# Second attention: the value products of the third group of heads placed in the next unit's list loop

## The reference, cut to what matters

```
x = _layernorm(x + _L0_attn_ref(x, ...))      # 32 heads of 128, sliding window
x = _layernorm(x + _L0_ffn_ref(x, ...))
x = _layernorm(x + _L1_attn_ref(x, ...))      # the part that changes
x = _layernorm(x + _L1_ffn_ref(x, ...))

# _L1_attn_ref: 32 query heads of 16 columns, 8 key heads, so 4 query heads share a key head
draft = einsum('bhqd,bhkd->bhqk', qr, kr) + causal mask
_, draft_indices = top_k(draft, 128)          # 128 largest keys of each query row and head
mask = neg everywhere, 0 at draft_indices, neg above the diagonal
scores = einsum('bhqd,bhkd->bhqk', qr, kr) / sqrt(16) + mask
out = einsum('bhqk,bhkd->bhqd', softmax(scores), v) @ Wo.T
```

## Time and profile before

| | us |
|---|---|
| median of three runs | 2230.96 |
| the profiled execution | 2229.73 |
| its span | 2227.9 |
| busy in the span: TensorE | 1843.1 (83%) |
| VectorE | 1500.7 (67%) |
| ScalarE | 1181.9 (53%) |
| GpSimd | 802.1 (36%) |

### The profile page before, as it was taken

The page is one execution under the profiler, slowest core; times in us unless marked ns, Lnnn a source line. Parts: engine busy times, 40 slices in busy tenths (PEclk is TensorE's granted clock), DMA queues, the critical chain, the costliest instruction groups (busy, mean ns, idle before and its releaser), DMA issues. The chain is left out here.

```text
span 2227.9 us, 27786 instructions
## 1 busy us (share of the span) xinstructions
PE 1843.1 (83%) x8586; PEld 1325.6 (60%) x8600; DVE 1500.7 (67%) x3316; ACT 1181.9 (53%) x2969; POOL 802.1 (36%) x519
## 2 busy tenths in 40 slices
PE   5899899998999869999766677777777778667997
PEld 4777777777777657888653343333333344436885
DVE  3677777777777654555754678888888887822345
ACT  3556556565565433332435676877667766342221
POOL 3445455454554425654411211112321111123442
PEclk9999999999999979999875888889888887787998
DMA  4011121111210112231221000010000000001111
GB/s 162 26 54 56 42 96 44 53 52 45 96 44 25 62 57 85 85 111 59 80 92 51 15 15 15 15 29 13 16 15 15 15 9 8 14 15 48 43 42 52
DMA packets 49490, 104.11 MB, mean 47 GB/s; under 512 B 6768, under 2 KB 31728, under 8 KB 45296
## 3 DMA queue, kind: packets, MB, share of 16 engines
q1 hardware_dynamic: 49392, 102.95, 13.6%
HBM read 95.59 MB, written 7.34 MB: 46 GB/s over the span
## 5 line engine op out<-in xcount | busy, mean ns | idle before, releaser
L230 PE MATMUL PS<-XT,AR 128*128 128x512 f32 x2472 | 621.5, 406 | 26.2 <-POOL AR L838 12.3
L230 PE MATMUL PS<-AR 128*128 128x512 f32 (+2 forms) x2568 | 540.0, 364 | 24.2 <-POOL AR L347 13.1
L230 PEld LDWEIGHTS PS<-XT,AR 128*128 128x128 f32 x2472 | 472.1, 193 | 140.2 <-issue 17.0
L230 PEld LDWEIGHTS PS<-AR 128*128 128x128 f32 x2568 | 440.9, 192 | 116.6 <-POOL AR L347 16.2
L1536 POOL TENSOR_TENSOR AF<-AF 128x1024 f32<-128x1024 f32 (+3 forms) x56 | 140.1, 2502 | 598.0 <-DVE AF L1811 598.0
L1753 DVE MAX8 BF<-PS 128x8 f32<-128x256 f32 (+2 forms) x384 | 196.6, 555 | 59.8 <-PE PS L1295 53.4
L1448 ACT ACTIVATE AF<-PS 128x512 f32<-128x512 f32 x152 | 87.5, 594 | 217.8 <-PE PS L1306 149.4
L1320 PE MATMUL PS<-AF,BF 128*128 128x512 f32 x304 | 175.8, 683 | 24.7 <-ACT AF L1448 24.6
L591 POOL TENSOR_TENSOR AF<-AF 128x512 f32<-128x512 f32 (+1 forms) x64 | 107.5, 1680 | 167.9 <-DVE AF L722 167.9
L585 POOL TENSOR_TENSOR AF<-AF 128x512 f32<-128x512 f32 x80 | 103.1, 1289 | 170.6 <-ACT AF L377 170.6
L558 ACT ACTIVATE AF<-AF 128x256 f32<-128x256 f32 (+1 forms) x256 | 120.3, 471 | 64.5 <-DVE AF L716 64.5
(11 more groups left out here) (213 smaller groups left out, 3484.1 us busy)
## 6 DMA issues: line engine op xcount, KB each, us to landing
AF<-in_mean_w SPq DMA_DIRECT2D x48, 448.0 KB, 3.3
AF<-in_ffn_w SPq DMA_DIRECT2D x14, 1536.0 KB, 6.5
AF<-in_attn_w SPq DMA_DIRECT2D x9, 1536.0 KB, 7.0
XT<-rope_scratch SPq DMA_DIRECT2D x174, 64.0 KB, 2.7
AF<-in_attn_w SPq DMA_DIRECT2D x9, 1024.0 KB, 5.2
AF<-in_ffn_w SPq DMA_DIRECT2D x11, 769.0 KB, 4.2
rope_scratch<-BF SPq DMA_DIRECT2D x20, 256.0 KB, 2.3
AF<-in_x SPq DMA_DIRECT2D x8, 256.0 KB, 4.3
```

Source lines behind the costliest of these rows:

```text
L230: last = nc.tensor.matmul(dst, lhs(a, c), rhs(m, c), start=(first and k == 0), stop=(k == 3 * n - 1 and not more))
```

## The change

On TensorE the value steps of group 2 leave the unit's own value phase (`q < 3` becomes `q < 2`) and stand in the next unit's list loop ahead of those of group 3: step s of the two groups together stands behind head s, for s from 0 to 2(i+2)-1. On ScalarE the copies of group 2 leave the end of the value phase, and the copies of both groups stand one before every two heads of the first count, in place of one before every four. On VectorE the first update stands behind head 8, where it stood behind head 6. The second update stays behind head 14.

```
@@ pe_attn1
-                    if 0 <= xp - 1 < NB and h <= tile_of(xp - 1)[1] + 1:
-                        values(xp - 1, 3, h)
+                    if 0 <= xp - 1 < NB:
+                        steps = tile_of(xp - 1)[1] + 2
+                        if h < 2 * steps:
+                            values(xp - 1, 2 + h // steps, h % steps)
...
-                    if 0 <= xp < NB and q < 3:
+                    if 0 <= xp < NB and q < 2:
                         for kb in range(tile_of(xp)[1] + 2):
                             values(xp, q, kb)
@@ act_attn1
-                for k in range(4):
-                    if 0 <= xp - 1 < NB and k <= tile_of(xp - 1)[1]:
-                        pt(xp - 1, 3, [k])
+                for k in range(8):
+                    if 0 <= xp - 1 < NB and k < 2 * (tile_of(xp - 1)[1] + 1):
+                        pt(xp - 1, 2 + k // (tile_of(xp - 1)[1] + 1), [k % (tile_of(xp - 1)[1] + 1)])
                     if search:
-                        count(x, 0, range(4 * k, 4 * k + 4))
+                        count(x, 0, range(2 * k, 2 * k + 2))
...
                     pt(xp, 1)
                     exp(xp, 3)
-                    pt(xp, 2)
@@ dve_attn1
-                    if search and h in (6, 14):
-                        update(x, (h - 6) // 8)
+                    if search and h in (8, 14):
+                        update(x, (h - 8) // 6)
```

## The result

The changed kernel takes 2299.74 us, the median of four runs (2295.11 to 2300.96), beside 2233.1 us for the kernel before on the same chip (2230.54 to 2236.7). The ratio is 1.0294, interval 1.0275 to 1.0313: slower by 66.6 us. I had forecast +48 us (2277) and a range up to 2296. Direction and most of the mechanism came out, the size did not, and one cost was missing from the sum.

What follows compares the result with a forecast made beforehand. List loops were taken as bound by TensorE for the first i+2 heads, then VectorE; value phases by VectorE's chain. 28.8 us for order plus 19 for clock on 2229.7 gave 2277.5, forecast 2277, range 2262 to 2292 (2252 to 2296 with rivals).

Steps and rivals of the forecast that it cites:

- Group 2 out of the value phase: 0.: Value phase: VectorE's chain ends it and needs no group 2, so nothing is won; TensorE only waits longer.
- The added steps and the chain through ScalarE.: List loops: 34 steps of 1.36 us and a later last copy delay both updates; unit 5's cut +4.0 us.
- the replay: Step-by-step timing of each list loop under the new order, giving unit 7 4.2 us and unit 10 3.
- The term of 28.8: Sum over the list loops of what the new order costs, without the clock: 28.8 us.
- Fewer copy waits: 1 to 1.3 us a loop.: List loops: with a copy before every two counts, products stop waiting for ScalarE's copies, worth 1 to 1.3 us a loop.
- Loops where a tile ends.: `o_lo` behind head 7 waits for the last product; VectorE stands 5.4 us in unit 6; loops +4.5 (unit 6), +6.9 (unit 8).
- rival 3: Low clock lasts two spells instead of one, another 3 us on six or seven loops: 2297 us; chance 0.12.
- The clock at the start: 19 us.: Longer waits ahead of the lists start nearly every list loop at the low clock: 19 us, bounds 0 and 36.
- Rival 2: List loops: the added steps fill TensorE's 36.3 us of waits for picks, so the kernel gets faster, 2222 us; chance 0.04.
- Rival 4: No change: slack behind head 9 hides the cost, units 3 to 8 lose under 1 us each, 2230 to 2237; chance 0.03.
- My argument against the page: Value phases of the kernel before: twelve restarts at low clock lose 12 x 3.3 = 40 us, 1.8% of the span.

Runs made afterwards that it cites:

- the shorter filling: Changed kernel plus 6(i+1) unread 128x512 matmuls on TensorE behind group 1 of the values, units 0 to 10: 2287.32 us; with `o_lo` behind head 10: 2265.73 us.
- the longer filling: Changed kernel with `o_lo` behind head 10 and 8(i+1) unread 128x512 matmuls behind group 1 of the values: 2256.74 us, ratio 1.0113.
- light steps: Changed kernel with group 2 cut to one transpose a step and products of 4 columns, copies full size: 2285.05 us, ratio 1.0253.
- the spread projection: Kernel before with filling matmuls ahead of the value phases and the projection split into four pieces behind heads 9 to 12: 2223.48 us, ratio 0.9962.

## Why the prediction failed in its size

The 66.6 us taken apart by the medians: with `o_lo` behind head 10 -17.5 (2282.2), with the clock up at every loop's start a further -25.5 (2256.7), and 23.9 are left. Taken each against the kernel before that was timed beside it, the parts are 20.3, 22.5 and 23.9 us. They also depend a little on the order: the shorter filling gave 12.4 us with `o_lo` behind head 7 and 16.5 us with it behind head 10.

- *Group 2 out of the value phase: 0.* Right. Value phases +1.4 us together; TensorE only waits longer for the first mark (71.5 us without unit 0, and I had said about 70).
- *The added steps and the chain through ScalarE.* Right in mechanism and about right in size. In unit 5's loop at full clock the price is 39.4 - 35.6 = 3.8 us; I had 4.0. In unit 3 it is 4.0 (I had 3.3), in unit 4 1.4 (0.9). In units 7 and 10 the replay does not fit: the loops are 0.7 us longer and 2.1 us shorter than before, where I had 4.2 and 3; but both started at a low clock in the kernel before, so their comparison is not at equal clock. The term of 28.8 also held the stand at `o_lo`; without it 23.9 us remain, and beside them stand the waits at the updates (30.5 us instead of 8.3).
- *Fewer copy waits: 1 to 1.3 us a loop.* The waits shrank (24.6 to 15.7 us), and alone this was worth nothing (ratio 1.0018); that the clock eats the gain fits units 6 and 8 but is not shown.
- *Loops where a tile ends.* **This is the step that failed.** I had the stand itself right (unit 6: forecast 5.4, measured 5.54), and said that the rest is "VectorE's own pace". It is not: behind the stand TensorE's clock falls a second time and the projection, 12 matmuls in a lump, runs into it. That added 9.3 us of waits in units 2, 4, 6 and 8 and was in no term of the sum. With the 4.8 us of stands in units 2, 4 and 10 (below) it covers the 12.5 us that these loops were over the forecast. It is the two spells of rival 3, to which I gave 0.12. TensorE did wait for picks, as rival 3 says, but for picks held up by `o_lo`, and the second spell came in four loops and not in six or seven. That its 2297 lies so near the measured 2299.74 is in part luck. Filling the gap took 5.8 us of it away in units 6 and 8 (3.0 and 2.8) without touching the stand. In units 2 and 4 the filling could not be made without being in the way. With `o_lo` behind head 10 the wait behind unit 2's projection fell from 4.18 to 1.03 us, but that edit takes the stand away too, so in these two units the cause is only argued.
- *The stand in units 2, 4 and 10.* Left out of the sum; measured 1.03, 2.05 and 1.74 us. The low clock at the start does not make them: with the first filling unit 10 starts at 1.00 and stands 1.74 us all the same. So these are errors of the replay, and I have not traced them further.
- *The clock at the start: 19 us.* Right: the longer filling won 25.5 us in the time and 25.6 in the loops, inside the bounds of 0 and 36, and 6.5 of the latter are units 7, 8 and 10 (1.5, 1.6 and 3.3), for which I had taken nothing, since they start low in the kernel before (0.61 to 0.64). In the other eight loops it is 19.2 us. In these three the filling lifts the clock above that of the kernel before, so I count much of the 6.5 us not as a price of the change, and the order's own price lies correspondingly above 23.9 us, up to some 30.
- *Rival 2 (TensorE's gaps take the steps).* Refuted: the picks' waits rose from 53.4 to 87.0 us. *Rival 4.* Refuted by units 3 to 8. The Trainium skill's "Perfetto Trace Analysis", section "Optimization Strategy", says that interleaving regimes whose most contended engines differ may improve performance. It did not here: a step of 1.36 us met a gap of 0.55 us, and the kernel took 23.9 us more than before even with the clock up at the starts and `o_lo` out of the way.

The Trainium skill, "TensorE: Matmul & The Clock Gate", section "What's actually happening", puts the ramp penalty under 1% of a typical kernel's span. I read that as nothing of note, which was wrong: my own 19 us were 0.85% of the span. The runs give 22.5 to 25.5 us for the starts, 1.0 to 1.1%, too near to decide. My argument against the page, 12 restarts of 3.3 us each, does not hold as a time either: with TensorE filled ahead of the value phases the kernel was 0.16% faster (interval 0 to 0.32%), not 1.8%. So TensorE's lost work there is mostly not the kernel's lost time.

What stays open: how the 23.9 us split between TensorE's added work and ScalarE's chain (the kernel with light steps moved the clock as well), why the clock falls in one loop and stays up in another with about the same work ahead of it, and how often the clock at a loop's start falls in the executions that were timed without a profile.

## What to carry to other kernels

Work taken out of an engine's wait can cost more than its own duration when the wait was keeping something else alive: here TensorE's group 2 filled a gap ahead of every list loop, and taking it away made most of the loops start at a low clock (0.50 to 0.79). When moving a step, compare its length with the gap behind one step of the host loop, and follow every instruction in an in-order queue (here `o_lo`) that waits for the moved work's end, and then what its waiting leaves idle. Price a clock fall at every place where TensorE becomes idle, and look at what stands first behind it in one lump.

## What the runs showed of the hardware that I had not expected

- Less work made the kernel slower: 2252.9 us against 2235.9 with group 2 nearly empty, the granted clock at unit 5's loop 0.50 instead of 1.00.
- A single wait in the middle of a busy loop can cost the clock. In unit 6's loop TensorE waited 3.51 us, and the 7 us from 1661 had 0.53; with 20 matmuls in that gap the projection took 3.02 us instead of 4.96. With the finer copies alone the clock fell in unit 8's loop behind waits of up to 1.07 us, while the kernel before kept 1.00 behind waits of up to 0.97.
- Filling work is not free. Where 20 matmuls met a stand of only 1 us (unit 2), the loop grew by 3.4 us.
- A higher clock is not yet time: the filling in the value phases brought the mean over the second attention from 0.85 to 0.92 and the time down by 0.16% only (0 to 0.32%); the same 0.92 with the spread projection by 0.38% (0.22 to 0.54%).
